# An RNN, a gated cell and their norms on one core: the second pass regrouped into tiles of one batch and eight steps

## The chip, the cores and the metric

The kernel runs on 1 core of one Trainium2 chip. The metric is the device time of one execution in microseconds (us). Engines are named PE (TensorE), DVE (VectorE), ACT (ScalarE), POOL (GpSimd) and SP (SyncE, which issues all DMAs here).

## The reference, cut to what matters

```python
mod = (_silu(c) @ wmod).reshape(8, 6, 1, 256)          # sa, ca, ga, sb, cb, gb
ga = (2 * (ga >= 0) - 1) * jnp.maximum(jnp.abs(ga), 0.25)   # the same for gb
h = _layernorm(x) * (1 + ca) + sa                      # x is [8, 1024, 256] float32
xb = h @ B.T
# over 1024 time steps, for 8 batches at once:
s = jnp.tanh(s @ A.T + xb_t);  y_t = s @ C.T
x = x + ga * (_layernorm(y + h) * gamma + beta)
h = _layernorm(x) * (1 + cb) + sb
# over the 8 batches as a scan, for all 1024 positions at once, c starts at in_c:
ft = sigmoid(h @ wf.T + c @ uf.T + bf);  it = sigmoid(h @ wi.T + c @ ui.T + bi)
gt = tanh(h @ wc.T + c @ uc.T + bc);     c = ft * c + it * gt
x = x + gb * jnp.tanh(h @ wo.T + c_final @ uo.T + bo)
```

## The kernel before, in words

The 1024 steps are cut into K=16 chunks of L=64 steps. One column of a tile is one (batch, chunk), so a step of the recurrence treats 8 x 16 = 128 columns. Since the chunks run side by side, the kernel makes a first pass to find each chunk's starting state, and a second pass that computes the output; a test at the end repeats both if a starting state was not good enough.

**First pass** (`unit1`, 36 units, one pair of steps each). Every unit norms two steps of x, adds the shift (POOL L511), transposes them (PE L1120), writes them to `h_park` in HBM, multiplies them by B (PE L1102, 12 matmuls) and keeps the result in `state`. From step `SKIP`=8 on, 28 units also carry two steps of the recurrence: PE L1062, DVE add L794, ACT tanh L612.

**Second pass** (`unit2`, 53 units). Unit u runs recurrence steps 2u and 2u+1 (u < 32), multiplies the states by C (L1164 in float32, L1173 from unit 10 in three high and low part products), adds `htok` (DVE L859) and norms the result twice (`bn_stats`, `bn_aggr`, reciprocal root as `ve` and a power on POOL L554/L556 and L546/L548). The transposes (L1253) put the features on the partitions; ACT L673 and DVE L909 write their high and low parts into the rings `hi` and `lo`. After eight pairs (GROUP=8) have been collected, the units from G0=11 on do the gates, one batch of 256 positions each: three gates of 12 matmuls from `hi`/`lo` (`gate_x`) and 12 from the cell state (`gate_c`, not for the first batch), all in L1136; ACT L705 applies the nonlinearities, POOL L532 and DVE L955, L854 form the new cell state `cst`, ACT L668 and DVE L864 its high and low parts `chi`, `clo`. From O0=19 on a unit multiplies one pair by wo (L1136, 12 matmuls), adds (DVE L936), takes tanh (ACT L693), scales by gb (POOL L567), transposes back (PE L1241, 4 transposes) and adds into `state` (DVE L947), which SP stores. In the first three groups of gates this is spread over the gate units of the next group; the last group's follows after the last gates.

The order of work on each engine is the order in which `unit2` of that engine names it; nothing is reordered at run time. Loops of two units are used in the stretches where all units are alike (`walk`), with registers in the addresses; the other units are written out. `has(u, first, n)` means first <= u < first + n.

Of the kernel before, what the change touches and what calls it, by code (L numbers as in the profile page):

```python
# [3 lines left out]

class At:
# [5 lines left out]
    def lin(self, k, c0=0):  # L21

        c = k * self.c + c0
        return c if isinstance(self.i, int) else self.i * (2 * k) + c

    def half(self, k, back, c0=0):

        c = k * ((self.c - back) // 2) + c0
        return c if isinstance(self.i, int) else self.i * k + c


def adaln_kernel(nc, x, A, B, C, gamma, beta, wf, uf, bf, wi, ui, bi, wc, uc, bc, wo, uo, bo, in_c, cond, wmod, out):
# [7 lines left out]
    P = 128  # L40
# [4 lines left out]
    SKIP = 8  # L45
# [34 lines left out]
    with ctx:  # L80
# [5 lines left out]

# [25 lines left out]
        hi = sb("hi", [P, 2, H, NB, GC], f32r)  # L112
        lo = sb("lo", [P, 2, H, NB, GC], f32r)
        xin = sb("xin", [P, 2, W])
        htok = sb("htok", [P, 2, W])
        h2tok = sb("h2tok", [P, W])
        y = sb("y", [P, W])[:, :]
        ow = sb("ow", [P, W])[:, :]
        pre = sb("pre", [P, D])
        hs = sb("hs", [P, 2, H, P])  # L120
        hs_hi = sb("hs_hi", [P, 2, H, P], f32r)
        hs_lo = sb("hs_lo", [P, 2, H, P], f32r)
        h_skip = sb("h_skip", [P, D])
# [45 lines left out]
        ga = state[:, at:at + D]  # L169
        gmag = state[:, at + D:at + 2 * D]  # L170
        gs = state[:, at + 2 * D:at + 2 * D + H * NB].rearrange("p (k b) -> p k b", k=H)
        gm = state[:, at + 3 * D:at + 3 * D + H * NB].rearrange("p (k b) -> p k b", k=H)
# [6 lines left out]
        BANK = dict(zip(NAMES, (psI, psG, psI, psG, psO, psI, psG, psO, psI, psG, psO)))  # L179

        def place(name):


            before = [i for i in range(NAMES.index(name)) if BANK[NAMES[i]] is BANK[name]]
            last = before[-1] if before else None
            return last, sum(n in whi for n in NAMES[:last + 1]) if before else 0

        def nth_split(name):

            return sum(n in whi for n in NAMES[:NAMES.index(name)])  # L190

        def whole(name):


            if name == "B":
                return state[:, 0:W].rearrange("p (k d) -> p k d", k=H)
            if name == "C":
                return ow.rearrange("p (k d) -> p k d", k=H)
            return (cst, uvec)[LATE.index(name) % 2][:, :, :]

        def ow_of(u):
            return ow if u < TAIL else (y, h2tok[:, :], ow)[(u - TAIL) % 3]

        def psW_of(u):
            return psW if u < TAIL else (psF, psG, psW)[(u - TAIL) % 3]

        def psO_of(u):
            return psO if u < TAIL else (psI, psO)[(u - TAIL) % 2]  # L210

        def back_of(u):

            back = 1 if u <= TAIL else 2
            return back if has(u, O0 + back, PAIRS) and u != TAIL + 1 else None

# [3 lines left out]
        q_w = {n: sem("q_w_" + n) for n in NAMES}  # L220
# [7 lines left out]
        q_wlo = sem("q_wlo")  # L228
        q_sig = sem("q_sig")
# [5 lines left out]
        q_tables = sem("q_tables")  # L235
        q_uc0 = sem("q_uc0")
# [1088 lines left out]
```

## Time and profile before

| | |
|---|---|
| median of 3 runs | 633.06 us (632.99 to 633.32) |
| the profiled execution, span from first to last instruction | 630.0 us |
| what lies around the span, median less span | 3.1 us |
| PE busy | 597.1 us, 95% |
| DVE, ACT, POOL busy | 462.2, 306.2, 368.7 us |
| HBM read and written | 29.90 and 16.78 MB, 74 GB/s over the span |

A page's busy time is the union of the spans of the instructions of an engine; it counts neither semaphore waits nor the issuing of DMAs. The matmuls of the page overlap in the pipeline, so what one costs is read from the distance between two starts in the timeline.

### The profile page before, as it was taken

The numbers are of one execution on the slowest core, as the hardware profiler recorded it, in microseconds if no ns is written. First come the engines' busy times: TensorE is split into PE (matmuls) and PEld (weight loads), VectorE is DVE, ScalarE is ACT, GpSimd is POOL, SyncE is SP. The second block draws the span as 40 slices with busy tenths as digits, with TensorE's granted clock in tenths as the row PEclk, the third lists the DMA queues.
The fourth block names the chain that finished last, engine by engine and source line by source line (L and its number), as shares of the span: only waits on it lengthen the run. The fifth ranks groups of instructions, "written<-read, shape, count | busy, mean of one in ns | idle before, by whom it ended". The sixth has DMA issues, their size and how long they took to land.

```text
span 630.0 us, 15433 instructions
## 1 busy us (share of the span) xinstructions
PE 597.1 (95%) x4840; PEld 580.0 (92%) x4840; DVE 462.2 (73%) x1143; ACT 306.2 (49%) x781; POOL 368.7 (59%) x479
## 2 busy tenths in 40 slices
PE   6699999999778899999999999999999999999995
PEld 3699999998668799999999999999999999999994
DVE  4799999956999988788778877777887672333335
ACT  2477777764443446535444454444445344333332
POOL 3666666643887576766676667776667533222234
PEclk9699999999999999999999999999999999999998
DMA  6644444432322212111111112111112000000003
GB/s 216 185 134 133 133 134 146 142 130 69 102 84 79 62 62 63 38 33 53 47 34 53 52 57 81 63 51 52 51 50 67 19 18 34 35 17 33 17 35 133
DMA packets 28557, 47.25 MB, mean 75 GB/s; under 512 B 4184, under 2 KB 7264, under 8 KB 28512
## 3 DMA queue, kind: packets, MB, share of 16 engines
q1 hardware_dynamic: 28512, 46.69, 22.9%
q8 instruction: 24, 0.39, 0.3%
q14 instruction: 21, 0.17, 0.1%
HBM read 29.90 MB, written 16.78 MB: 74 GB/s over the span
## 4 chain that ended last, share of the span: by engine, by line
PE 70%; DVE 10%; issue 9%; POOL 7%; DMA 1%; ACT 1%; SPq 0%; POOLq 0%; DVEq 0%; ACTq 0%
PE psF L1136 11%; PE psG L1136 11%; PE psI L1136 11%; PE psR L1062 10%; PE psW L1136 5%; PE psF L1062 4%; PE psC L1173 4%; PE psO L1102 4%; PE psW L1102 3%; PE psO L1241 1%; DVE state L917 1%; PE psT L1253 1%; POOL h2tok L526 1%; POOL gi L532 1%; DVE cst L854 1%
## 5 line engine op out<-in xcount | busy, mean ns | idle before, releaser
L1062 PE MATMUL psR<-hs,AT 128*128 128x128 f32 x648 | 109.0, 282 | 0.0
L1062 PEld LDWEIGHTS psR<-hs,AT 128*128 128x128 f32 x648 | 90.2, 194 | 3.5 <-ACT hs L650 0.2
L854 DVE TENSOR_TENSOR cst<-gf,gi 128x512 f32<-128x512 f32 x32 | 27.7, 865 | 62.9 <-POOL gi L532 62.9
L532 POOL TENSOR_TENSOR gi<-gi,gg 128x512 f32<-128x512 f32 x32 | 41.3, 1290 | 43.7 <-ACT gg L705 43.5
L567 POOL TENSOR_TENSOR ow<-ow,gbT 128x256 f32<-128x256 f32 x52 | 31.3, 622 | 60.8 <-ACT ow L693 60.8
L511 POOL TENSOR_TENSOR htok<-htok,uvec 128x256 f32<-128x256 f32 x64 | 46.1, 741 | 35.2 <-ACT htok L637 35.2
L1062 PE MATMUL psF<-hs,AT 128*128 128x128 f32 x312 | 61.2, 278 | 0.0
L518 POOL TENSOR_TENSOR hs_lo<-hs,hs_hi 128x256 fp32r<-128x256 f32 x44 | 42.5, 966 | 29.2 <-ACT hs_hi L658 29.1
L608 ACT ACTIVATE hs<-pre 128x256 f32<-128x256 f32 x42 | 17.6, 418 | 81.5 <-DVE pre L788 81.4
L955 DVE TENSOR_TENSOR gf<-gf,cst 128x512 f32<-128x512 f32 x28 | 28.7, 1027 | 33.2 <-ACT gf L705 33.2
L539 POOL TENSOR_TENSOR xin<-xin,gab 128x512 f32<-128x512 f32 x32 | 47.3, 1477 | 5.3 <-DMA xin<-in_L_attn_x_dram 5.3
L526 POOL TENSOR_TENSOR h2tok<-h2tok,sbt 128x512 f32<-128x512 f32 x32 | 48.9, 1528 | 0.0
L1062 PEld LDWEIGHTS psF<-hs,AT 128*128 128x128 f32 x312 | 48.3, 195 | 0.1
L917 DVE SCALAR_TENSOR_TENSOR state<-y,rstd,xin 128x256 f32<-128x256 f32 (+1 forms) x64 | 43.5, 718 | 0.4 <-POOL rstd L556 0.4
L612 ACT ACTIVATE hs<-pre 128x128 f32<-128x128 f32 x112 | 29.0, 305 | 29.4 <-DVE pre L794 29.3
L830 DVE SCALAR_TENSOR_TENSOR htok<-xin,mv,uvec 128x256 f32<-128x256 f32 x64 | 40.7, 674 | 1.8 <-DMA h_park<-htok 1.3
L668 ACT ACTIVATE chi<-cst 128x512 fp32r<-128x512 f32 x28 | 17.7, 632 | 49.9 <-DVE cst L854 49.9
L1136 PE MATMUL psI<-hi,wiT_hi 128*128 (+1 forms) x128 | 38.3, 299 | 0.0
L1136 PE MATMUL psF<-hi,wfT_hi 128*128 (+1 forms) x128 | 38.2, 298 | 0.0
L673 ACT ACTIVATE hi<-psT 128x256 fp32r<-128x256 f32 (+1 forms) x64 | 20.8, 377 | 33.5 <-PE psT L1253 33.5
L864 DVE TENSOR_TENSOR clo<-cst,chi 128x512 fp32r<-128x512 f32 x28 | 29.1, 1039 | 9.9 <-ACT chi L668 9.3
L1136 PE MATMUL psF<-hi,wfT_lo 128*128 (+1 forms) x128 | 36.3, 284 | 0.0
(255 smaller groups left out, 2326.9 us busy)
## 6 DMA issues: line engine op xcount, KB each, us to landing
xin<-in_L_attn_x_dram SPq DMA_DIRECT2D x64, 256.0 KB, 2.8
h_park<-htok SPq DMA_DIRECT2D x32, 256.0 KB, 2.0
htok<-h_park SPq DMA_DIRECT2D x32, 256.0 KB, 3.0
out_dram<-state SPq DMA_DIRECT2D x32, 256.0 KB, 2.0
state<-in_L_wmod_dram SPq DMA_DIRECT2D x3, 512.0 KB, 6.1
state<-in_L_attn_B_dram SPq DMA_DIRECT2D x1, 256.0 KB, 4.9
state<-in_L_attn_A_dram SPq DMA_DIRECT2D x1, 256.0 KB, 5.3
state<-in_L_attn_C_dram SPq DMA_DIRECT2D x1, 256.0 KB, 7.1
```

The lines of the kernel that those rows point to most:

```text
L511: pool.tensor_tensor(h, h, sa, ALU.add).then_inc(a_h, 1)
L518: pool.tensor_tensor(hs_lo[:, tt, :, :], hs[:, tt, :, :], hs_hi[:, tt, :, :].bitcast(f32), ALU.subtract).then_inc(s_hsl, 1)
L526: pool.tensor_tensor(h2, h2, sbt[:, :].rearrange("p (o d) -> p o d", o=1).broadcast_to([P, 2, D]), ALU.add).then_inc(s_h2, 1)
L532: pool.tensor_tensor(gi[:, :, :], gi[:, :, :], gg[:, :, :], ALU.mult).then_inc(s_ig, 1)
L539: pool.tensor_tensor(xg, xg, gab[:, :].rearrange("p (o d) -> p o d", o=1).broadcast_to([P, 2, D]), ALU.add).then_inc(s_xg, 1)
L567: pool.tensor_tensor(o4, o4, g4, ALU.mult).then_inc(s_ob, 1)
L830: dve.scalar_tensor_tensor(halfw(dst, tt), halfw(src, tt), mv[:, tt, 0:1], ca1, ALU.subtract, ALU.mult).then_inc(a_tmp, 1)
L854: dve.tensor_tensor(cst[:, :, :], gf[:, :, :], gi[:, :, :], ALU.add).then_inc(s_c, 1)
L917: dve.scalar_tensor_tensor(row(v.lin(1, -1), tt * D, D), halfw(y, tt), rstd[:, tt:tt + 1], halfw(xin[:, bk, :], tt), ALU.mult, ALU.add).th ...
L1062: ins = pe.matmul(ps, AT[:, k, m * P:(m + 1) * P], hs[:, 1 - tt, k, :], start=(k == 0 and (apart or m == 0)), stop=(k == H - 1 and (apart ...
L1102: last = pe.matmul(ps[:, m * 2 * P:(m + 1) * 2 * P], w["B"][:, k, m * P:(m + 1) * P], h[:, (ref - back) % 2, k * 2 * P:(k + 1) * 2 * P], s ...
L1136: last = pe.matmul(ps[:, at + m * columns:at + (m + 1) * columns], w[name][:, k, m * P:(m + 1) * P], xx(k), start=(start and n == 1), stop ...
```

## The change

A tile of the second pass is now one batch and 16 steps of all 16 chunks (`TB`=16, two halves j of `HT`=8 steps), 256 positions with the positions on the partitions, so that batch rows and outputs need no regrouping. The state of the recurrence is kept for four steps in `hs` and its parts for 16 steps in `hsh`, `hsl`; a C product (`project`) takes two batches and eight steps. The lags are CL=4 (C product), ML=8 (first norm), XL=10 (gates), OL=19 (output); NU=32 tiles, units 0 to 52, all written out. The product with wo follows in the gate unit itself, with the positions on the output's partitions, and waits in `wx` (11 buffers) for the cell's last state; the transposes back are gone. The identity matmuls that added `xb` (L1067) become DVE adds in units 0 to 9. Scale and shift of the second norm move into the copies after the transposes (`cb1T`) and into the biases (`shifts()` in unit 8: 6 and 72 matmuls). The norms' affine work moves from DVE to ACT (`zn`, `xn2`) and POOL (`zn` times a row). Rows of one batch come by broadcast DMAs from `rows_d`. All weights are loaded in the first pass. SKIP is 16: 24 of the 36 units of the first pass carry the recurrence, units 6 to 29.

The diff, cut to the order of the work on each engine. Four `unit2` follow one another: POOL's, ACT's, DVE's and PE's. What is left out of ACT's ahead of `step(2 * u + 1)`: tanh of step 2u, a late weight's copy, `xn2` (two, after `s_nB`), `chi` (after `s_c`), the tanh of `wx` (after `s_ua`); at its end the gates' sigmoids and tanh. Left out of DVE's ahead of `cst`: `nmB` (after `s_rB`), the add of step 2u, a late weight's difference; behind `x1`: `bn_stats` into `stB` and `bn_aggr` into `mvB`, each waiting for the one before.

```diff
-    SKIP = 8
+    SKIP = 16
-    LOADS = {1: ["B", "A", "wmod", "C"], 2: ["affine"], 3: ["wf"], 4: ["wi"], 5: ["wc"], 6: ["bias"]}
+    LOADS = {1: ["B", "A", "wmod", "C"], 2: ["affine"], 3: ["wf"], 4: ["wi"], 5: ["wc"], 6: ["bias"],
+             7: ["uf"], 8: ["ui"], 9: ["uc", "tabs"], 10: ["wo"], 11: ["uo"]}
...
+            def unit2(u):
+                if has(u, ML + 1, NU):
+                    m = u - ML - 1
+                    pool.wait_ge(s_mvB, 2 * m + 2)
+                    pool.tensor_tensor(veB[:, :], mvB[:, :, 1], epst[:, :], ALU.add).then_inc(s_veB, 1)
...
+                    pool.tensor_tensor(rstdB[:, :], veB[:, :], mhalf[:, :], ALU.pow).then_inc(s_rB, 1)
+                if has(u, XL + 1, NU):
...
+                    pool.wait_ge(s_g, 2 * n + 2)
+                    pool.tensor_tensor(gi[:, :, :], gi[:, :, :], gg[:, :, :], ALU.mult).then_inc(s_ig, 1)
+                if has(u, OL, LAST):
...
+                    pool.tensor_tensor(t, t, uvec[:, :], ALU.add).then_inc(s_ua, 1)
+                if has(u, ML, NU):
...
+                    pool.tensor_tensor(xg, xg, both(tA[:, m % 2, D:W]), ALU.add).then_inc(s_xg, 1)
+                    pool.wait_ge(s_mvA, 2 * m + 2)
+                    pool.tensor_tensor(veA[:, :], mvA[:, :, 1], epst[:, :], ALU.add).then_inc(s_veA, 1)
...
+                    pool.tensor_tensor(rstdA[:, :], veA[:, :], mhalf[:, :], ALU.pow).then_inc(s_rA, 1)
+                if has(u, 0, PAIRS):
+                    pool.wait_ge(s_hsh, u + 1)
...
+                    pool.tensor_tensor(pair_of(hsl[:, j], t), pair_of(hs, 2 * u % 4), pair_of(hsh[:, j], t).bitcast(f32),
+                                       ALU.subtract).then_inc(s_hsl, 1)
+                if has(u, ML, NU):
...
+                    pool.wait_ge(s_zn, 2 * m + 2)
+                    pool.tensor_tensor(two(zn[:, :]), two(zn[:, :]), both(tA[:, m % 2, 0:D]), ALU.mult).then_inc(s_zg, 1)
+                if has(u, OL, NU):
...
+                    pool.tensor_tensor(t, t, both(tG[:, o % 2, :]), ALU.mult).then_inc(s_ob, 1)
...
+            def unit2(u):
...
+                if has(u, 0, PAIRS):
+                    step(2 * u + 1)
...
+                    act.activation(pair_of(hsh[:, j], t), pair_of(hs, 2 * u % 4), ACT.Copy).then_inc(s_hsh, 1)
+                if has(u, XL - 1, NU):
...
+                    act.wait_ge(s_T, m + 1)
+                        act.activation(hi[:, m % 2, k, :], psT[:, k * POS:(k + 1) * POS], ACT.Copy,
+                                       scale=cb1T[:, k, m % NB:m % NB + 1]).then_inc(s_hi, 1)
+                if has(u, ML, NU):
+                    act.wait_ge(s_nA, m + 1)
+                        act.activation(zn[:, j * D:(j + 1) * D], tiles_of(m)[:, j, :], ACT.Identity, bias=nmA[:, j:j + 1],
+                                       scale=rstdA[:, j:j + 1]).then_inc(s_zn, 1)
...
+            def unit2(u):
...
+                if has(u, XL + 1, NU):
+                    dve.wait_ge(s_ig, n + 1)
+                    dve.tensor_tensor(cst[:, :, :], gf[:, :, :], gi[:, :, :], ALU.add).then_inc(s_c, 1)
+                if has(u, CL, 8 * NT):
+                    dve.tensor_tensor(z, (psC, psO)[c % 2][:, :], hin[:, c % 3, :], ALU.add).then_inc(s_z, 1)
+                        dve.bn_stats(stA[:, T % 2, 2 * (b + i) + j, :], halfw(z, i)).then_inc(s_stA, 1)
+                if has(u, XL + 1, NU) and (u - XL - 1) % NB < NB - 1:
+                    dve.tensor_tensor(clo[:, :, :], cst[:, :, :], chi[:, :, :].bitcast(f32), ALU.subtract).then_inc(s_clo, 1)
+                if has(u, OL + 1, NU):
+                    dve.tensor_tensor(tiles_of(o), tiles_of(o), two(wx[:, o % NWX, :]), ALU.add).then_inc(s_fin, 1)
+                if has(u, 0, PAIRS):
+                    step(2 * u + 1)
+                if has(u, ML, NU):
+                        dve.bn_aggr(mvA[:, j, :], stA[:, m // NB % 2, 2 * (m % NB) + j, :]).then_inc(s_mvA, 1)
+                if has(u, XL - 1, NU):
+                    dve.wait_ge(s_hi, 2 * m + 2)
+                        dve.scalar_tensor_tensor(lo[:, m % 2, k, :], psT[:, k * POS:(k + 1) * POS], cb1T[:, k, m % NB:m % NB + 1],
+                                                 hi[:, m % 2, k, :].bitcast(f32), ALU.mult, ALU.subtract).then_inc(s_lo, 1)
+                if has(u, ML, NU):
+                    dve.wait_ge(s_rA, m + 1)
+                    dve.scalar_tensor_tensor(nmA[:, :], mvA[:, :, 0], -1.0, rstdA[:, :], ALU.mult, ALU.mult).then_inc(s_nA, 1)
+                if has(u, XL, NU):
+                    dve.tensor_tensor(two(wx[:, n % NWX, :]), two(psW[:, :]), both(tW[:, n % 2, :]), ALU.add).then_inc(s_wx, 1)
+                if has(u, ML, NU):
+                    dve.wait_ge(s_zg, m + 1)
+                    dve.tensor_tensor(tiles_of(m), two(zn[:, :]), two(xin[:, m % 2, :]), ALU.add).then_inc(s_x1, 1)
...
+                if has(u, XL, NU):
+                    dve.wait_ge(s_f, 2 * n + 2)
+                    dve.tensor_tensor(gf[:, :, :], gf[:, :, :], prev, ALU.mult).then_inc(s_fc, 1)
...
+            def unit2(u):
...
+                    step(2 * u)
+                    late(u)
+                    project(u - CL)
+                    gate_x(n, 0)
+                    gate_x(n, 1)
+                    step(2 * u + 1)
+                    tokens(n + 1)
+                    gate_x(n, 2)
+                    times_uo(n // NB - 1)
+                    times_wo(n)
+                    shifts()
+                        gate_c(n, i)
```

## Rows read from the trace of the kernel before

**Rows 1.** The page, busy time, share of the span and instructions of each engine.

```profile
PE 597.1 (95%) x4840; PEld 580.0 (92%) x4840; DVE 462.2 (73%) x1143; ACT 306.2 (49%) x781; POOL 368.7 (59%) x479
```

**Rows 2.** Busy time by stretch: PE, weight loads, DVE, ACT, POOL; PE clock, DMA share, GB/s.

```profile
160.00:180.00 20.00, 16.39 (x120) 14.58 (x120) 19.89 (x53) 10.26 (x30) 16.32 (x21) 1.00 0.39 120
340.00:360.00 20.00, 20.00 (x174) 20.00 (x173) 16.77 (x42) 8.34 (x21) 13.46 (x17) 1.00 0.13 41
```

**Rows 3.** Timeline of PE, one full unit: start, duration, line, op, out<-in, count.

```profile
402.31 0.28 PE L1136 MATMUL psF<-chi,ufT_hi 128*128 128x256 f32 x1
...
406.57 1.05 PE L1062 MATMUL psR<-hs,AT 128*128 128x128 f32 x8
407.38 0.37 PE L1173 MATMUL psC<-CT_hi,hs_hi 128*128 128x256 f32 x1
...
409.65 0.60 PE L1241 MATMUL psO<-ident,ow 128*128 128x128 f32 x4
410.00 0.36 PE L1136 MATMUL psF<-hi,wfT_hi 128*128 128x256 f32 x1
...
423.69 0.60 PE L1241 MATMUL psO<-ident,ow 128*128 128x128 f32 x4
```

**Rows 4.** Timeline of DVE, ACT and POOL, same unit; the last row from the groups by shape.

```profile
409.76 0.69 DVE L859 TENSOR_TENSOR y<-psC,htok 128x512 f32<-128x512 f32 x1
409.88 0.63 ACT L668 ACTIVATE chi<-cst 128x512 fp32r<-128x512 f32 x1 [0.73 <-DVE cst L854]
...
412.15 0.24 DVE L872 BATCH_NORM_AGGREGATE mvb<-stb 128x2 f32<-128x6 f32 x2
412.31 0.72 DVE L878 BATCH_NORM_STATS2 st<-y 128x6 f32<-128x256 f32 x2
412.47 0.20 POOL L546 TENSOR_TENSOR ve<-mvb,epst 128x2 f32<-128x2 f32 x1 [0.79 <-DVE mvb L872]
412.74 0.70 POOL L548 TENSOR_TENSOR rstdb<-ve,mhalf 128x2 f32<-128x2 f32 x1
...
414.83 0.41 DVE L788 TENSOR_TENSOR pre<-psR,state 128x256 f32<-128x256 f32 x1
415.17 0.74 DVE L909 TENSOR_TENSOR lo<-psT,hi 128x256 fp32r<-128x256 f32 x2
415.36 0.42 ACT L608 ACTIVATE hs<-pre 128x256 f32<-128x256 f32 x1 [2.56 <-DVE pre L788]
...
416.14 0.90 ACT L690 ACTIVATE h2tok<-h2tok,rstdb 128x256 f32<-128x256 f32 x2
...
421.82 1.29 POOL L532 TENSOR_TENSOR gi<-gi,gg 128x512 f32<-128x512 f32 x1 [0.17 <-ACT gg L705]
...
L673 ACT ACTIVATE hi<-psT 128x256 fp32r<-128x256 f32 x36 | 11.8, 378 | 27.5 <-PE psT L1253 27.5
```

**Rows 5.** Timeline: a DVE operation with two SBUF inputs beside a POOL operation.

```profile
410.40 1.28 POOL L539 TENSOR_TENSOR xin<-xin,gab 128x512 f32<-128x512 f32 x1
410.61 1.62 DVE L864 TENSOR_TENSOR clo<-cst,chi 128x512 fp32r<-128x512 f32 x1 [0.17 <-ACT chi L668]
```

**Rows 6.** Timeline and chain, PE: the second pass's start, and the c0 block.

```profile
139.82 0.38 PE L1062 MATMUL psR<-hs,AT 128*128 128x128 f32 x2
...
196.12 0.22 PE psR L1062 x2
...
198.32 4.20 PE psW L1136 x36
202.52 0.63 PE psR L1062 x2
```

**Rows 7.** Timeline of DVE: first and last of 32 cell states, last output add.

```profile
230.57 1.13 DVE L854 TENSOR_TENSOR cst<-gf,gi 128x512 f32<-128x512 f32 x1 [1.61 <-POOL gi L532]
...
606.40 0.69 DVE L854 TENSOR_TENSOR cst<-gf,gi 128x512 f32<-128x512 f32 x1 [3.34 <-POOL gi L532]
...
625.20 0.69 DVE L947 TENSOR_TENSOR state<-psO,state 128x512 f32<-128x512 f32 x1 [1.23 <-PE psO L1241]
```

More of the change, by code:

```diff
@@ L119, in adaln_kernel @@
+        gf = sb("gf", [P, H, POS])
+        gi = sb("gi", [P, H, POS])
+        gg = sb("gg", [P, H, POS])
+        cst = sb("cst", [P, H, POS])
+        chi = sb("chi", [P, H, POS], f32r)
+        clo = sb("clo", [P, H, POS], f32r)
+        uvec = sb("uvec", [P, W])
+        tA = sb("tA", [P, 2, W])
+        tW = sb("tW", [P, 2, D])
+        tG = sb("tG", [P, 2, D])
         pre = sb("pre", [P, D])
-        hs = sb("hs", [P, 2, H, P])
-        hs_hi = sb("hs_hi", [P, 2, H, P], f32r)
-        hs_lo = sb("hs_lo", [P, 2, H, P], f32r)
@@ L146, in adaln_kernel @@
         again = sb("again", [1, 1], i32)
-        EARLY = ["B", "A", "C"]
-        NAMES = EARLY + LATE
+        htok = hin
+        st = stA[:, 0, 0:2, :]
+        mv, ve, rstd = mvA, veA, rstdA
+        whi["B"], wlo["B"] = chi, clo
+        sbE_hi, sbE_lo = chi[:, :, 0:P], clo[:, :, 0:P]
+        ca1, sa = uvec[:, 0:D], uvec[:, D:W]
+        hmT_hi, hmT_lo = (r[:, 0, 0, :, :, :].rearrange("p (i c) t k -> p i (c t k)", i=2) for r in (hsh, hsl))
         at = RAW * W
@@ L168, in adaln_kernel @@
         at += W
[L169 to L172, printed above, removed]
+        ga, gmag, gs, gm = (state[:, at + i * D:at + (i + 1) * D] for i in range(4))
         def bank(name):
@@ L178, in adaln_kernel @@
             "psR", "psC", "psT", "psF", "psI", "psG", "psW", "psO"))
[L179 to L190, printed above, removed]
-        def whole(name):
[L195 to L215, printed above, removed]
+        BANK = {"B": psI, "A": psG, "C": psI}
+        LBANK = (psG, psW, psI)
+        def whole(name):
+            return (state[:, 0:W] if name == "B" else zn[:, :]).rearrange("p (k d) -> p k d", k=H)
         q_ident = sem("q_ident")
         q_table = sem("q_table")
-        q_w = {n: sem("q_w_" + n) for n in NAMES}
+        q_w = {n: sem("q_w_" + n) for n in EARLY + LATE}
         q_wm = [sem(f"q_wm{j}") for j in range(3)]
@@ L408, in load @@
                                  allow_slow_non_contiguous=True).then_inc(q_bias, 16)
+                elif what == "tabs":
+                    sp.wait_ge(q_tab, 16)
+                    for i in range(3):
+                        sp.dma_start(rows_d[:, i, :], rows[0:P:K, i, :]).then_inc(q_rows, 16)
                 else:
@@ L1288, in unit2 @@
-                gate_c(1)
-                gate_c(2)
+                if x and n % NB:
+                    for i in range(3):
+                        gate_c(n, i)
             def body():
```

1072 lines of the change are left out of this document (552 added, 520 removed).

## The prediction, made before the changed kernel was run

> **What bounds the kernel now.** I read the page's busy times first: PE stands at 95% of the span, no other engine above 73% [rows 1]. Then the busy times by stretch, to see where that isn't so: between 160 and 180 us, in the first units of the second pass, DVE is busy 19.89 of 20 us and PE only 16.39; by 340 us PE is busy all the time at full clock, and DVE has 3 us of slack, POOL 6.5 [rows 2]. The timeline of PE shows one full gate unit from 409.65 to 423.69, so 14.04 us, back to back [rows 3]: 36 products of a gate pass take 4.26 (402.31 to 406.57), a recurrence step 0.81, the four transposes back 0.35, and the product behind such a group starts some 0.09 late. The gates run from the first cell state at 230.57 to the last at 606.40, 375.8 us [rows 7]: that is the bulk, and PE sets it. The profiled execution spans 630.0 us and the median is 633.06, so 3.1 us come on top of any span below.
>
> **What the change does to PE.** Transposes back: 4 per pair, 0.35 + 0.09 = 0.44 us, gone 32 times: -14 us where PE sets the pace. The full unit then takes 14.04 - 0.44 = 13.60. A first-batch unit has no `gate_c` (-4.26), and units 18, 26 and 34 add the uo product (about 1.75, an estimate from its 4 float32 matmuls at twice the columns of half a recurrence step's 4). Units without recurrence save 1.8, without C product 1.42 (12 at a third of 4.26). From unit 11 to 41 PE's work sums to 13.6 x 21 + 11.8 x 4 + 10.4 x 6 - 3 x 4.26 + 3 x 1.75 = 387.7. It is more than the 375.8 before, since the first group's wo products, once behind the gates, now stand in front.
>
> **What paces a unit then.** The order on DVE, ACT and POOL is fixed, so I follow what each waits for in a full unit, from one cell state to the next. All durations from [rows 4] but for the cell state's 0.69 [rows 7]; "to" is the 0.03 to 0.17 between an end and the start that it releases.
> (a) DVE: cst 0.69, z (as y L859) 0.69, to 0.16, statistics 0.72, clo 0.69, output add 0.69 (two SBUF inputs, as cst), add of step 2u+1 0.41: 4.15 with gaps. chi on ACT is hidden by z and its statistics.
> (b) ACT: to 0.12, tanh 0.42, hsh 0.63 (512 elements, as chi), hi 0.72 (two of 0.378); DVE: to 0.15, lo 0.86, nmA 0.17: 3.15. The mean's way (aggregate 0.24, ve 0.20, power 0.70) runs beside it.
> (c) ACT: to 0.12, zn 0.90 (as L690, two); POOL: to 0.07, zn times row 1.28; DVE: to 0.10, x1 0.69: 3.16.
> (d) DVE: to 0.16, statistics 0.74, aggregate 0.34: 1.24.
> (e) POOL: to 0.08, ve 0.20, to 0.07, power 0.70; then gi times gg 1.29 and 0.10 to the next cst: 2.44. The power stands ahead of the gate product in POOL's queue, so the next cell state waits for this unit's norm. That closes the ring.
> Sum 14.15 us a unit, more than PE's 13.60, though no engine is busy more than about 10 of them.
>
> **Where two engines meet.** A `clo` that starts while POOL is at a 1.28 us operation takes 1.62 instead of 0.69: POOL's ends at 411.68, DVE's 0.55 later, at 412.23 [rows 5]; so a DVE operation with two SBUF inputs finishes 0.55 after POOL's end. In the ring this comes three times. POOL goes from gi straight to the uvec add (or the `xg` add), 0.1 ahead of cst: +1.05. It goes from the zn product straight to the gb product, ahead of x1: +1.05. And DVE goes from the aggregate straight to gf, ahead of ve: +0.55. Bounds: nothing to 2.65; I take all, since in each case both are ready at that instant. Ring: 16.8 us a unit.
> The Trainium skill (SBUF - State Buffer, two separate sides) calls the pair of ports that VectorE and GpSimd share an exclusive lock, held by who starts first; the rows agree in the end time, and by a bandwidth split instead the ring would stay nearer 15.5.
>
> **The sum over the gate units.** Units 19 to 31: 13 x 16.8 = 218.4. Units 11 to 18 have no output add (-0.7) and no gb product (-1.05): 8 x 15.05 = 120.4. Units 32 to 35 without recurrence: (b) shrinks to lo and nmA behind the power, -2.0: 4 x 14.8 = 59.2. Units 36 to 39 without z, but with the wait for chi (0.63 and two gaps): 4 x 14.1 = 56.4. Units 40, 41 have no first norm, PE sets 10.6: 21.2. Three units without clo: -2.2. Together 473.4 from the first cell state to the last, against 375.8: **+97.6**.
>
> **Ahead of it.** First pass: four units (30 to 33) drop the recurrence. Each drops four DVE adds of at most 0.41 and 1.6 of PE, but its chain ve, power, scale, two shifts on POOL stays at some 3.4 of the 3.8 us that a unit takes: 0 to 6.6 in all, I take -2.5. Five more weights (256 KB each) and `tabs` on SP's queue I cost at nothing: SP only issues, and the copies are wanted 15 units later; if the link were full, about 1 us each. The second pass starts at 139.82 [rows 6], so now at 137.3. Units 0 to 3: one step is PE 0.8, two half adds, two half tanh, then the weight's copy and difference stand between the steps: 3.85 each. Units 4 to 7 add the C product between the steps and z, statistics on DVE behind it: 5.4 each. Unit 8: step, C product, step, then `shifts`. The 36 tiny c0 products took 4.20 [rows 6], so 78 take some 9.2, and the granted clock suffers: the pair of recurrence matmuls behind the c0 block took 0.63 and not 0.22. Unit 8 is 12.6 with 1 for that clock. Units 9 and 10 run the ring's parts (a) to (e) without the cell state: 11.5 each. To the first cell state at unit 11, with (e): 15.4 + 21.4 + 12.6 + 23 + 2.5 = 75, so 212.3 against 230.57: **-18.3**. DVE's three full norm operations that moved to ACT and POOL are part of that gain.
>
> **Behind it.** Last cell state to the end is 23.6 now [rows 7]. Then: cst 0.7, uo 1.9, its copy 0.7, first add 0.8, tanh and gb product 2.1, and eight outputs each with two DVE adds and one POOL product that exclude each other (0.69 + 0.69 + 1.28, less where tanh hides: 2.5 each), last add to the end 4.1 as today (625.89 to 630.0): 29. **+5.3**.
>
> Span 212.3 + 473.4 + 29 = 714.7; time 717.8, say **718 us**, 13% slower.
>
> **Unrolling.** PE is busy 20.00 of 20 us in the looped stretch [rows 2], so loops cost no time there and writing them out gives none. The Trainium skill (Runtime: NRT & Kernel Launch, instruction fetch mechanics) says a taken branch outside the window stalls on a fetch; by it the looped stretches would give back perhaps a few us; this trace shows no such gap on PE.
>
> **Rivals.**
> 1. The ring closes within PE's time (something I put in series runs beside it, so the ring is under 13.6): PE stays the bound. Units 11 to 41 take 387.7, the ramp stays near 75 or, if its ring parts are shorter too, 62, the end 25: span 137.3 + 62 to 75 + 387.7 + 25 = 612 to 625, time 615 to 628. It would be **faster**. For it: PE is at 95% today and loses 14 us of work; DVE loses two norm passes. Against it: the ring needs only seven handovers with durations measured here, and even without meeting POOL it sums to 14.15. It decides at a mean of 12.6 us per unit for the 31 units (630 less what lies around them).
> 2. The ring is there, but the meetings cost less (POOL's next operation comes after DVE's, or the lock is short): 14.15 in units 19 to 31, PE's 13.6 in 11 to 18, 12.1 and 11.4 in 32 to 39: 184 + 109 + 48 + 46 + 21 = 408, and an end of 25: span 645, time 648. With one of the meetings, 665 to 690.
> 3. The DMAs are late: twice as many rows of 1 KB, and three broadcasts a unit, some 1.3 MB. At 16 us a unit that is 80 GB/s, and the stretch from 160 us moves 120 [rows 2]; loads are issued a unit or two ahead. If they were late the time would be above 740.
> 4. The change does nothing to the pace, gains and losses cancel within 0.2%, about what a measurement of this kernel can tell from no change.
>
> **How the numbers follow.** The ring with its meetings 0.55 (own range 695 to 738), the ring with fewer of them 0.23 (645 to 695), PE-bound 0.16 (612 to 630), late DMAs or more 0.04, no difference 0.02. The range 648 to 738 leaves out the PE-bound case and the tail above. Faster is rival 1, 0.16; same 0.02; slower is the rest, 0.82.
>
> **What would show it.** PE's busy share near 80% and long regular gaps on PE in front of `gate_c`, ended by DVE clo; a unit of 16 to 17 us between two `cst`; `cst` and `x1` at about 1.7 us each where POOL is at an add; POOL's gi product starting right behind the power, and long after ACT's last tanh; the first `cst` near 212 us. Wrong if units are 13.6 us apart with PE back to back, or if gi waits for ACT's gg as today (421.82, idle ended by ACT [rows 4]).

## The result and the profile after

The changed kernel takes 718.28 us (median of 4 runs, 716.79 to 720.45) beside 633.19 for the kernel before on the same chip: a ratio of 1.135 (95% interval 1.1328 to 1.1373), 85 us slower. The profiled execution took 716.79 us and spans 715.0; TensorE's mean granted clock is 0.924 (before 0.982).

The page of the kernel after: busy time, share of the span and instructions; then the chain that ended last, by engine; then groups of PE, DVE and POOL with their idle time before and what ended it.

```profile
PE 592.8 (83%) x4650; PEld 571.7 (80%) x4650; DVE 477.1 (67%) x1062; ACT 340.7 (48%) x804; POOL 394.9 (55%) x453
...
POOL 32%; issue 25%; PE 17%; DVE 15%; ACT 5%; DMA 3%; SPq 2%; POOLq 0%; DVEq 0%; ACTq 0%
...
L1128 PE MATMUL psR<-hs,AT 128*128 128x128 f32 x432 | 69.6, 295 | 42.3 <-ACT hs L655 32.5
...
L878 DVE TENSOR_TENSOR cst<-gf,gi 128x512 f32<-128x512 f32 x32 | 49.9, 1560 | 7.6 <-POOL gi L549 6.9
...
L865 DVE SCALAR_TENSOR_TENSOR nmB<-mvB,rstdB 128x2 f32<-128x2 f32 x32 | 37.5, 1172 | 25.4 <-POOL rstdB L544 25.4
L581 POOL TENSOR_TENSOR wx<-wx,tG 128x512 f32<-128x512 f32 x32 | 41.8, 1308 | 20.1 <-DMA tG<-rows_d 11.6
```

PE has 4 us less work than before [rows 1] in 85 us more, and its recurrence matmuls (L1128) alone have 42.3 us of idle time ahead of them, 32.5 of it ended by ACT. No engine is near its limit; "issue" and POOL hold the chain. The cell add takes 1.56 us in the mean, and `nmB`, an operation on two columns, 1.17.

The busy times by stretch say the same of the middle (columns as in [rows 2]). PE waits, its clock dips, and no other engine is full.

```profile
400.00:420.00 20.00, 15.47 (x127) 15.06 (x127) 14.27 (x25) 9.27 (x21) 14.15 (x14) 0.97 0.34 104
440.00:460.00 20.00, 16.87 (x137) 16.29 (x136) 12.62 (x25) 10.63 (x26) 13.23 (x13) 1.00 0.30 92
```

One unit, from a cell add (L878) to the next: 497.16 to 513.08, 15.92 us. DVE's timeline (start, duration, line, op, out<-in, count, idle before and what ended it):

```profile
497.16 1.50 DVE L878 TENSOR_TENSOR cst<-gf,gi 128x512 f32<-128x512 f32 x1
...
503.64 0.88 DVE L919 SCALAR_TENSOR_TENSOR lo<-psT,cb1T,hi 128x256 fp32r<-128x256 f32 x2 [1.80 <-ACT hi L691]
504.43 0.15 DVE L925 SCALAR_TENSOR_TENSOR nmA<-mvA,rstdA 128x2 f32<-128x2 f32 x1
...
507.11 1.76 DVE L934 TENSOR_TENSOR state<-zn,xin 128x512 f32<-128x512 f32 x1 [1.92 <-POOL zn L575]
509.01 0.75 DVE L938 BATCH_NORM_STATS2 stB<-state 128x6 f32<-128x256 f32 x2
509.94 0.25 DVE L943 BATCH_NORM_AGGREGATE mvB<-stB 128x2 f32<-128x6 f32 x2 [0.17 <-DVE stB L938]
510.10 0.66 DVE L950 TENSOR_TENSOR gf<-gf,cst 128x512 f32<-128x512 f32 x1
511.62 1.21 DVE L865 SCALAR_TENSOR_TENSOR nmB<-mvB,rstdB 128x2 f32<-128x2 f32 x1 [0.86 <-POOL rstdB L544]
512.75 0.41 DVE L857 TENSOR_TENSOR pre<-psR,state 128x256 f32<-128x256 f32 x1
513.08 1.50 DVE L878 TENSOR_TENSOR cst<-gf,gi 128x512 f32<-128x512 f32 x1
```

POOL's in the same unit, and one row of ACT's:

```profile
505.79 1.28 POOL L575 TENSOR_TENSOR zn<-zn,tA 128x512 f32<-128x512 f32 x1 [1.55 <-ACT zn L698]
507.03 1.29 POOL L581 TENSOR_TENSOR wx<-wx,tG 128x512 f32<-128x512 f32 x1
510.26 0.55 POOL L541 TENSOR_TENSOR veB<-mvB,epst 128x2 f32<-128x2 f32 x1 [1.95 <-DVE mvB L943]
510.89 0.69 POOL L544 TENSOR_TENSOR rstdB<-veB,mhalf 128x2 f32<-128x2 f32 x1
511.55 1.26 POOL L549 TENSOR_TENSOR gi<-gi,gg 128x512 f32<-128x512 f32 x1
512.76 1.26 POOL L555 TENSOR_TENSOR wx<-wx,uvec 128x512 f32<-128x512 f32 x1
```

```profile
507.04 0.85 ACT L714 ACTIVATE gg<-psG,biasT 128x256 f32<-128x256 f32 x2
```

The reader should see three things. ACT finishes `gg` at 507.89, and POOL takes it up only at 511.55, since `veB` and the power stand ahead in its queue and wait for the norm's statistics. `x1` (L934) and `cst` (L878) take 1.76 and 1.50 us where POOL has just begun an operation of its own. And `nmB` is held from 511.62 to 512.83 by `gi` on POOL.

The second pass in four stretches, in us (before from [rows 6, 7]; after from the timelines of PE and DVE):

| stretch | before | after | difference |
|---|---|---|---|
| start of the pass | 139.82 | 141.42 | +1.6 |
| to the first cell add | 90.75 | 83.79 | -7.0 |
| first to last cell add | 375.8 | 453.5 | +77.7 |
| to the end | 23.6 | 36.3 | +12.7 |
| span | 630.0 | 715.0 | +85.0 |

### The profile page after: what moved, and what is told of

It is laid out like the page before. It is cut to its first block, busy times and chain, and to the rows that moved or that the text cites. A ratio compares the mean times of both kernels' runs of the same rounds, so it can differ in the third digit from the quotient of the medians.

```text
span 715.0 us, 13830 instructions
## 1 busy us (share of the span) xinstructions
PE 592.8 (83%) x4650; PEld 571.7 (80%) x4650; DVE 477.1 (67%) x1062; ACT 340.7 (48%) x804; POOL 394.9 (55%) x453
## 4 chain that ended last, share of the span: by engine, by line
POOL 32%; issue 25%; PE 17%; DVE 15%; ACT 5%; DMA 3%; SPq 2%; POOLq 0%; DVEq 0%; ACTq 0%
POOL zn L575 6%; POOL gi L549 6%; POOL xin L561 4%; POOL wx L581 4%; POOL wx L555 3%; DVE cst L878 3%; POOL hsl L570 3%; POOL veB L541 2%; PE psR L1061 2%; PE psO L1092 2%; PE psF L1061 2%; POOL rstdA L566 2%; DVE hin L835 2%; PE psW L1092 2%; PE psW L1243 1%
## 5 line engine op out<-in xcount | busy, mean ns | idle before, releaser
L1128 PE MATMUL psR<-hs,AT 128*128 128x128 f32 x432 | 69.6, 295 | 42.3 <-ACT hs L655 32.5
L1128 PEld LDWEIGHTS psR<-hs,AT 128*128 128x128 f32 x432 | 58.4, 201 | 49.4 <-ACT hs L655 36.9
L934 DVE TENSOR_TENSOR state<-zn,xin 128x512 f32<-128x512 f32 x32 | 44.6, 1395 | 56.5 <-POOL zn L575 56.5
L575 POOL TENSOR_TENSOR zn<-zn,tA 128x512 f32<-128x512 f32 x32 | 41.1, 1286 | 48.0 <-ACT zn L698 48.0
L531 POOL TENSOR_TENSOR hin<-hin,uvec 128x256 f32<-128x256 f32 x64 | 46.5, 748 | 34.3 <-ACT hin L642 34.3
L570 POOL TENSOR_TENSOR hsl<-hs,hsh 128x512 fp32r<-128x512 f32 x32 | 41.0, 1282 | 33.7 <-ACT hsh L684 32.2
L878 DVE TENSOR_TENSOR cst<-gf,gi 128x512 f32<-128x512 f32 x32 | 49.9, 1560 | 7.6 <-POOL gi L549 6.9
L581 POOL TENSOR_TENSOR wx<-wx,tG 128x512 f32<-128x512 f32 x32 | 41.8, 1308 | 20.1 <-DMA tG<-rows_d 11.6
L561 POOL TENSOR_TENSOR xin<-xin,tA 128x512 f32<-128x512 f32 x32 | 50.4, 1574 | 0.0
L1161 PE MATMUL psG<-hi,wcT_hi 128*128 128x256 f32 x128 | 43.4, 339 | 0.0
L835 DVE SCALAR_TENSOR_TENSOR hin<-xin,mvA,uvec 128x256 f32<-128x256 f32 x64 | 40.9, 679 | 2.4 <-DMA h_park<-hin 0.8
L1161 PE MATMUL psG<-lo,wcT_hi 128*128 128x256 f32 x128 | 40.2, 314 | 0.0
L1161 PE MATMUL psG<-hi,wcT_lo 128*128 128x256 f32 x128 | 40.1, 313 | 0.0
```

The source lines that it names most:

```text
L531: pool.tensor_tensor(h, h, sa, ALU.add).then_inc(a_h, 1)
L561: pool.tensor_tensor(xg, xg, both(tA[:, m % 2, D:W]), ALU.add).then_inc(s_xg, 1)
L570: pool.tensor_tensor(pair_of(hsl[:, j], t), pair_of(hs, 2 * u % 4), pair_of(hsh[:, j], t).bitcast(f32), ALU.subtract).then_inc(s_hsl, 1)
L575: pool.tensor_tensor(two(zn[:, :]), two(zn[:, :]), both(tA[:, m % 2, 0:D]), ALU.mult).then_inc(s_zg, 1)
L581: pool.tensor_tensor(t, t, both(tG[:, o % 2, :]), ALU.mult).then_inc(s_ob, 1)
L835: dve.scalar_tensor_tensor(halfw(dst, tt), halfw(src, tt), mv[:, tt, 0:1], ca1, ALU.subtract, ALU.mult).then_inc(a_tmp, 1)
```

## The experiments

All ran beside the kernel before, on the same chip as the others of their set. In the table is the median of 4 runs (7 for the first pass alone), and the ratio to the kernel before with its 95% interval. The kernel after has 718.28 and 1.135. Places in a trace are those of one profiled execution, so a few us of difference in the median need not all be found there.

| kernel | us | ratio |
|---|---|---|
| 1 ring reordered | 697.71 | 1.1011 (1.097 to 1.1053) |
| 2 gb product first | 717.94 | 1.1338 (1.1303 to 1.1374) |
| 3 hi first | 724.38 | 1.1435 (1.1398 to 1.1471) |
| 4 after, less of wo | 718.60 | 1.1362 (1.1317 to 1.1408) |
| 5 gb first, nm by scalars | 697.61 | 1.1038 (1.0991 to 1.1086) |
| 6 = 1 with 5 | 667.80 | 1.0568 (1.0497 to 1.064) |
| 7 before, first pass of the change | 629.24 | 0.9938 (0.9915 to 0.9962) |
| 8 after, shifts mostly left out | 712.32 | 1.1242 (1.1216 to 1.1269) |
| 9 bo's row later | 713.98 | 1.1253 (1.1216 to 1.129) |
| 10 last gamma rows early | 712.07 | 1.1228 (1.1194 to 1.1263) |
| 11 = 6, 9 and 10 | 661.11 | 1.0439 (1.0403 to 1.0475) |
| 12 before, less of wo | 625.52 | 0.9872 (0.9842 to 0.9901) |

**1. The order on POOL, DVE and ACT.**

```diff
 POOL
+   gi * gg            (waits for ACT's i and g)
    veB, rstdB         (wait for mvB)
-   gi * gg
 DVE
-   nmB                (waits for rstdB)
    pre (step 2u), cst
+   nmB
    z, statistics, clo
 ACT
+   chi                (waits for cst)
    xn2 (two, wait for nmB)
-   chi
```

> Three entries of the serial queues change places in the second pass, no work is added or left out: POOL multiplies i by g ahead of the variance and rstd of LayerNorm B; DVE's two-column nmB goes from the head of the unit to just behind the cell add; ACT copies chi ahead of the normalisation of the other batch. Theory (a ring through the in-order queues of DVE, ACT and POOL paces a unit, 15.94 us, and PE with 13.6 us of work does not): the path gates -> gi -> cell add -> chi -> gates loses about 1.7 us, the units 19 to 31 fall to 14.3, the units with no LayerNorm B meeting to about 13.7, some 39 us in all: 679 us. Rival, PE or its lower clock sets the unit: 716 to 720, no change. Rival, late loads set it: no change either. Rival, only the operation that is held longest matters and another takes its place at once: 705 to 715.

Measured 697.71 us, 21 less, where 679 was forecast. Most profiled cell adds are 14.20 us apart in units 19 to 31, against 15.94: the forecast 14.3 for that piece held, and with it the claim that `veB` and the power in front of `gi` lengthened the ring; PE's work is the same. The other half of the forecast failed: units 11 to 18 stayed at 14.2 instead of 13.7 and units 32 to 37 rose from some 14.0 to between 14.0 and 16.2. The chain of this kernel (start, duration, what) from 247 us on shows why: two queues now close another ring, gates, `gi`, `veB`, the power, a held `nmB`, `xn`, PE's transposes and gates.

```profile
247.25 0.85 ACT gg L714 x2
...
248.32 1.64 issue
249.96 0.19 POOL veB L546
250.23 1.12 POOL rstdB L549
251.37 1.24 DVE nmB L878
252.63 1.10 ACT xn L671 x2
...
253.78 0.66 PE psT L1196 x4
```

**2. One exchange on POOL.**

```diff
+   wx * tG            (gb product, output)
    zn * row           (waits for ACT's zn)
-   wx * tG
```

> One exchange on POOL: the output's product with tG goes ahead of LayerNorm A's product with the table row, so that POOL no longer works on two SBUF inputs while DVE wants to add x1. Theory (the ring runs through x1 and what stands behind it on DVE): x1 falls from 1.76 to about 0.7 us in 21 units (19 to 39), each unit 1.1 shorter, 23 us in all: 695 us. Rival, DVE's waits at x1 are slack that PE fills: 716 to 720. Rival, PE paces the unit: the same, 716 to 720.

Measured 717.94: nothing, the intervals overlap. Read alone this would speak for the first rival. DVE's timeline of this kernel, and POOL's, say something else:

```profile
503.99 1.08 DVE L925 SCALAR_TENSOR_TENSOR nmA<-mvA,rstdA 128x2 f32<-128x2 f32 x1
...
507.60 0.69 DVE L934 TENSOR_TENSOR state<-zn,xin 128x512 f32<-128x512 f32 x1 [1.93 <-POOL zn L581]
```

```profile
503.76 1.29 POOL L577 TENSOR_TENSOR wx<-wx,tG 128x512 f32<-128x512 f32 x1
506.28 1.29 POOL L581 TENSOR_TENSOR zn<-zn,tA 128x512 f32<-128x512 f32 x1 [1.23 <-ACT zn L698]
```

`x1` fell from 1.76 to 0.69 us as forecast, and the meeting moved: the gb product, started earlier, now holds `nmA`, 1.08 us for two columns instead of 0.15, with all of `zn` behind it. The units are 15.8 long.

**3. hi ahead of the hidden state's copy on ACT.**

```diff
+   hi (two, wait for psT)
    hsh copy
-   hi
```

> One exchange on ACT: the rounding of the new tile to hi goes ahead of the copy of the hidden state for the next project. Theory (the ring includes hi, since PE's gates wait for it): about 0.6 us less in 21 units, 11 us in all: 706 us. If hi is not on the ring, or PE paces: 716 to 720.

Measured 724.38, 6 us slower, units of 16.2. The same thing again: `hi` comes earlier, so that `lo` starts 5.83 us behind the cell add instead of 6.48, but `hsl` on POOL, which needs `hsh`, comes later and lies over `nmA`, which then takes 1.07 us (DVE's timeline of this kernel, and POOL's).

```profile
509.89 1.07 DVE L926 SCALAR_TENSOR_TENSOR nmA<-mvA,rstdA 128x2 f32<-128x2 f32 x1
```

```profile
509.65 1.29 POOL L570 TENSOR_TENSOR hsl<-hs,hsh 128x512 fp32r<-128x512 f32 x1 [0.64 <-ACT hsh L693]
```

**4 and 12. A third of wo's products left out, in the kernel after and in the kernel before.**

```diff
-                        for h, w in ((hi, whi), (hi, wlo), (lo, whi)):
+                        for h, w in ((hi, whi), (lo, whi)):
```

> The kernel after, with the product of wo's rounding rest left out (4 of its 12 matmuls in every tile, 0.47 us of PE per unit; the output lacks that term). Theory (ring): PE has 2.3 us to spare in a unit, the time stays within 1 us of the kernel after: 717 to 718.5. Rival, PE's work or clock sets the unit: 32 x 0.47 = 15 us less, 703 us.

> The kernel before, with the same third of wo's products left out as in the kernel after (where it gave 0.0 us; the output lacks that term). Theory: in the kernel before PE sets the pace of the second pass, so that nearly all of 32 x 0.47 = 15 us shows: 618 to 621 us. Rival, a ring through the other engines binds before as well: 630 to 633.

In the kernel after the cut gave nothing (718.60), in the kernel before 8.4 us (625.52 beside 633.91). So PE's work is no longer on the path after the change, and it was before. But not all of the 15 us came out before: freed of them, PE waits there too, 37.02 us busy in a stretch of 40 (first fence below) where the kernel before has 40.00, and from 312 us on the chain of the cut kernel runs through ACT's gates, POOL's `gi`, DVE's norm and adds and POOL again.

The kernel before has this ring itself. Its chain is PE alone from 300 to 426 us, but from 427 to 514 us it runs mostly through POOL (five of its rows in the second fence: start, duration, what). Its cell adds in units 19 to 21 and 27 to 29 are 13.6 us apart, just as in the cut kernel, and only those in 22 to 25 take the 13.9 to 14.1 of PE's work, which the cut brings down to 13.6. So a full unit of the kernel before can't get under 13.6 us by less work on PE: its ring lies 0.4 us under PE's 14.04.

```profile
460.00:500.00 40.00, 37.02 (x310) 36.23 (x309) 30.32 (x72) 17.12 (x43) 25.18 (x32) 1.00 0.13 45
```

```profile
448.46 1.29 POOL gi L532
449.86 1.14 DVE cst L854
451.02 0.64 ACT chi L668
...
456.74 1.00 POOL hs_lo L518
...
462.08 1.29 POOL gi L532
```

**5 and 6. The small operations in a form that isn't held.** 5 is experiment 2 with `nmA` and `nmB` as below; 6 has the order of experiment 1 as well.

```diff
-   dve.scalar_tensor_tensor(nmB[:, :], mvB[:, :, 0], -1.0, rstdB[:, :], ALU.mult, ALU.mult)
+   for j in range(2):
+       dve.tensor_scalar(nmB[:, j:j + 1], mvB[:, j, 0:1], rstdB[:, j:j + 1], -1.0, ALU.mult, ALU.mult)
```

> The exchange of the run before (gb product ahead of the zn product on POOL) moved the meeting from x1 (1.76 to 0.69 us) to the two-column nmA (0.15 to 1.08 us), and the units stayed at 15.8. Here nmA and nmB are made by two tensor_scalar operations each (the mean times a per-partition scalar, so one SBUF input instead of two), with that exchange. Theory (DVE operations with two SBUF inputs are held while POOL runs one with two, and such a hold sits on the ring): nmA and nmB take 0.1 to 0.3 us in all and are not held, the gain at x1 stays, the units 19 to 31 fall from 15.9 to 14.8, some 1 us in 21 units and a little in the rest: 718 to about 695. Rival, the small operations are held in this form too: 715 to 718, units 15.8. Rival, the two scalar operations cost more than they save: 720 and over.

> The reordering that gave 697.7 us (gi ahead of rstdB on POOL, nmB behind the cell add, chi ahead of xn) with the gb exchange and with nmA and nmB as tensor_scalar operations. Its profile showed a new ring of 14.2 us: gates, gi, veB, rstdB, nmB held for 1.2, xn, PE's transposes and gates. Theory: nmB not held takes 1 us out of that ring, it falls under PE's own work, and PE sets the unit with 13.6 to 13.8 us: 30 units by 0.5 and 7 by up to 1.5 in the last third, 697 to about 680 us. Rival, the small operations are held in this form too, or PE's work already set the 14.2: 695 to 698.

Measured 697.61 and 667.80. With one tensor input, not two, two operations of one column each take 0.33 us together, also while POOL is at work, so the holds are gone. The edits do not add up singly: against the kernel after the exchange on POOL alone is worth nothing, with the two forms 21 us, the order alone 21 us, all together 50. What the forms are worth without the exchange wasn't run. Units 19 to 31 are 15.04 apart in 5, near the forecast of 14.8, and 13.35 in 6, where I had put 13.6 to 13.8. In 6 the ring is under PE's work: the chain of that kernel has PE alone between 440 and 480 us (five of its rows in the second fence; the first is DVE's timeline), and PE is busy 40.00 us from 340 to 380.

```profile
441.00 0.33 DVE L928 TENSOR_SCALAR nmA<-mvA,rstdA 128x1 f32<-128x1 f32 x2
```

```profile
449.66 0.44 PE psT L1200 x4
450.09 1.38 PE psG L1165 x12
451.48 1.36 PE psW L1214 x12
452.84 1.41 PE psF L1165 x12
...
457.08 0.89 PE psR L1132 x8
```

**7. The first pass of the change in the kernel before.**

```diff
-    SKIP = 8
-    RAW = 8
+    SKIP = 16
+    RAW = 12
```

(and the loop's cuts as in the change)

> The kernel before with the first pass of the change alone: its side work starts from step 16 instead of 8 and fewer states are kept raw; the second pass is that of before. Theory: the first pass gets shorter by less than one unit's side work, 1.5 to 2 us: 631.2 to 631.7. Rival, the first pass is set by PE's recurrence and projection alone: no change, 633.2. Rival, all of the skipped side work counted, 6.6 us less: 626.6. Rival, the start of the second pass moves later, as in the kernel after (141.4 against 139.8): 635.

Measured 629.24 beside 633.16, and this is the only complete version here that is faster than the kernel before: by 0.4 to 0.9%. The gain by the median, 3.9 us, is twice the forecast 1.5 to 2. Its profiled execution was among the slower of its runs (631.36 of 627.63 to 631.38): there the second pass starts at 138.70 instead of 139.82, 1.1 us earlier. Where the rest comes from isn't shown.

**8. The bias shift.** Of the 72 eight-column matmuls 66 are left out (so the biases are not shifted as they should be).

```diff
-  for name, shi, slo in ((wf/wi/wc, sbT_hi, sbT_lo), (uf/ui/uc, c0z_hi, c0z_lo)): 12 matmuls per column block
+  one matmul per column block
```

> The kernel after with 66 of the 72 eight-column matmuls of the bias shift left out before unit 8 (the biases of the second pass are not what the reference wants). Their profile: 10.3 us for the second half, a granted clock of 0.67 in the 20 us from 180 on and 0.82 in the next 20, and the first gates 12.9 us later than I forecast. Theory (the matmuls cost their time and the half clock behind them): the first cell add comes 12 to 15 us earlier, 704 to 706 us. Rival, the clock falls there for another reason, the pause of PE, so that only the matmuls' own time goes: 708 to 710. Rival, another chain (LayerNorm, hi) is as late as they: 712 to 718.

Measured 712.32, 6 us less instead of 12 to 15, and the first cell add at 221.27 instead of 225.21. PE's next recurrence pair starts at 195.44, with the matmuls at 195.12: it waits 7.1 us for ACT, whose input waits in DVE's queue behind `nmB`. So the chain through the second norm ends as late as the matmuls, and what came forward is the C product behind them, from 196.83 to 186.67.

The granted clock between 180 and 200 us is 0.67 in both (half speed, 1.2 GHz, for part of the stretch), but it doesn't follow that the matmuls have no part in it. From some 180 to 184 us it is half in both, ahead of the matmuls; in the 20 us before, PE was busy 13.77 us in the one and 13.95 in the other, and whether those gaps are the cause wasn't tried. After that the two differ. With the matmuls the clock is full until 190.2 us and then half until 200.4: in the middle of them, and with PE busy without a pause since 180.4, their starts go from 0.11 to 0.21 us apart (first fence). Without them PE pauses from 188.3 to 195.4, and it is half from about 191 us to 200.4. A pause has taken their place, so the cause of that second fall stays open. The first two fences are from the kernel after, the others from this one.

```profile
190.11 0.25 PE L1243 MATMUL psW<-sbT_hi,wcT_hi 128*128 128x8 f32 x1
190.22 0.35 PE L1243 MATMUL psW<-sbT_lo,wcT_hi 128*128 128x8 f32 x1
190.43 0.35 PE L1243 MATMUL psW<-sbT_hi,wcT_lo 128*128 128x8 f32 x1
```

```profile
180.00:200.00 20.00, 19.59 (x121) 19.62 (x122) 6.29 (x19) 3.85 (x10) 7.05 (x9) 0.67 0.16 46
```

```profile
180.00:200.00 20.00, 12.30 (x73) 12.05 (x74) 9.54 (x26) 5.90 (x16) 8.82 (x12) 0.67 0.15 46
```

```profile
195.44 0.79 PE L1128 MATMUL psR<-hs,AT 128*128 128x128 f32 x2 [7.11 <-ACT hs L652]
```

**9. bo's row later in the first pass.**

```diff
-                    for dst, src in ((gamma_b, gamma), (beta_b, beta), (bo_b, bo)):
+                    for dst, src in ((gamma_b, gamma), (beta_b, beta)):
...
-             7: ["uf"]
+             7: ["bo", "uf"]
```

> The kernel after, with the broadcast of bo (128 KB) issued in unit 7 of the first pass instead of unit 2, where it stood ahead of the first x tile. In the kernel after, x landed 7.26 us after its issue and at 23.5, in the kernel before at 20.6, and the second pass began at 141.4 instead of 139.8. Theory: the first pass gets its 2.9 us back, the second pass begins at 138.5 to 139.2, 2.2 to 2.9 us less: 715.5 to 716. Rival, the first pass makes the late start up before its end: 718.

Measured 713.98, 4 us less than the kernel after. The second pass begins at 138.60, 2.8 us earlier, in the profiled execution; its first cell add comes 1.0 earlier, its span is 2.2 shorter. The broadcast of bo ahead of the first x tile (x landed 7.26 us after its issue, in 5.2 at most here) was what ate the gain of the shorter first pass. The kernel before has no such broadcast: it loads bo as 1 KB.

**10. The last six gamma rows early.**

```diff
+                if u == 38:
+                    sp.wait_ge(s_z, 8 * NT)
+                    six broadcasts rows_d -> hin
...
-                    pool.tensor_tensor(t, t, both(tG[:, o % 2, :]), ALU.mult)
+                    pool.tensor_tensor(t, t, both(row), ALU.mult)      # row in hin for the last six
```

> The kernel after, with the last six gamma rows of the output loaded early, into the tile hin that is no longer read by then, instead of one by one into the pair tG. Between the last cell add (678.69) and the end (715.0) the product on POOL waited for a row six times, 11.6 us in all. Theory: the drain falls from 36.3 us to 28 to 30, the time to 710 to 712. Rival, the drain is set by the rest of the chain (tanh, add, store): 716 to 718.

Measured 712.07, 6 us less; last cell add to the end 32.4 us instead of 36.3. The waits for the rows are gone, and my 28 to 30 was still too short: what is left is a cadence of 4.70 us for two tiles on POOL, each pair waiting 1.89 us for ACT's tanh, which waits for DVE's add, which waits behind an output add of 1.73. These are the rows of this kernel:

```profile
688.74 1.74 DVE L916 TENSOR_TENSOR state<-state,wx 128x512 f32<-128x512 f32 x1 [1.16 <-POOL wx L595]
...
691.82 2.81 POOL L595 TENSOR_TENSOR wx<-wx,hin 128x512 f32<-128x512 f32 x2 [1.89 <-ACT wx L691]
696.52 2.81 POOL L595 TENSOR_TENSOR wx<-wx,hin 128x512 f32<-128x512 f32 x2 [1.89 <-ACT wx L691]
```

**11. All of it.** No new lines, 6 with 9 and 10.

> All of the edits together: the reordered ring with unheld small operations (667.8 us, units of 13.35 us set by PE alone), bo's broadcast later and the last six gamma rows early. Theory: the gains add, since they lie in the three successive stretches: 667.8 less 2.5 less 7 = 658 us, and what is left over the kernel before (633) is the filling and draining of the second pass (80 and 28 us). Rival, the drain's rows come from the edge of the ring edit already: 663 to 666.

Measured 661.11, of a forecast 658. This is the best form of the second pass found here, 57 us faster than the kernel after and still 4.4% slower than the kernel before. In its profile the first cell add is at 217.95, the last at 627.12, the span 659.0: against the kernel before 12.6 us less ahead of the gates, 33.4 more between the cell adds and 8.3 more behind. Its units are 12.6 to 13.6 us up to unit 31. Units 19 to 31 are even shorter than before (172.6 against 178.5 us together), and 11 to 18, which now hold wo's products as well, are longer (105.7 against 95.8). The larger part of the 33.4 lies in units 32 to 41, 130.8 against 101.6: they take mostly 12.8 to 14.5 us each, the chain again goes through POOL's power, `xn` and PE, and the granted clock is 0.93 between 540 and 580 us. So most of what is left between the cell adds is the ring and the clock in the last ten units, not PE's work alone.

## Why the prediction was right

The time (718 against 718.28) and the span (714.7 against 715.0) came out nearer than the terms did: three errors of +12.9, -19.9 and +7.3 us cancel, and that is luck. The mechanism is the one given; the sizes need the list.

**The start.** "PE sets it", of the gates in the kernel before, holds only in part: a ring of 13.6 us stands right behind PE's 14.04 and paces six of its full units (12). The -14 us for the transposes was too much even for the old order: 15 us of PE's work gave 8.4 there.

**The ring.** Right, and shown: taking PE's work away does nothing (4), changing only the order takes 21 us (1), and with the holds gone as well PE sets the unit up to unit 31 (6). Size: 16.8 us a full unit forecast, 15.94 measured. By piece, forecast and measured: (a) 5.2 and 4.52, (b) 3.15 and 2.90, (c) 4.2 and 4.29, (d) 1.24 and 1.32, (e) 2.99 and 2.89. In (a), successive DVE operations overlap by about 0.08 us each in the trace, and `cst` took 1.50 and not 1.74: it starts 0.3 after POOL's uvec add, because a meeting that I had not listed stands before it. That is `nmB`, two columns, held until `gi` ends. I had priced it by its size. Units 11 to 18 were 14.2 in the mean (forecast 15.05), 32 to 35 14.1 and 36 to 39 13.7 (14.8, 14.1). Together the gates took 453.5 and not 473.4. Three durations of the sum are not in the rows that it names: lo 0.86 (0.74 there), nmA 0.17 and the aggregate's 0.34 (0.24 there); measured are 0.88, 0.15 and 0.25.

**The meetings.** All three were there: `x1` 1.76 us, `cst` 1.50, `veB` 0.55 instead of 0.20. They added 1.07, 0.81 and 0.35 us, 2.2 in place of 2.65. `x1` and `cst` ended 0.55 and 0.56 us after POOL's operation, as forecast (507.11 + 1.76 = 508.87, POOL's ended at 508.32). The 0.55 is not the same for every size: the two-column `nmB` ended 0.02 after POOL's `gi`, and POOL's `veB` 0.05 after DVE's `gf`. The Trainium skill (SBUF - State Buffer, two separate sides) has it that a DVE operation with two SBUF inputs and a GpSimd operation that reads SBUF exclude each other, and that the one that starts first holds the pair of ports for its whole length. The runs agree: `nmB` with two tensor inputs took 1.21 us, to the end of `gi`, and with one it took 0.33. What the prediction didn't say is that such a hold can't be priced one at a time: 2 and 3 each removed one delay and made another, in 2 nearly as large (1.07 and 0.93 us), in 3 larger (0.65 and 0.92).

**Ahead of the gates.** Wrong by 12.9 us (212.3 against 225.21), in three steps. "Each drops ... I take -2.5" was -1.1 in the kernel before (7, profiled start of the second pass); and bo's row, a load that the prediction's list leaves out, cost 2.8 us (9), so that the pass started 1.6 later instead of 2.5 earlier. "Unit 8 is 12.6 with 1 for that clock" was 17.1: step, C product and step took 5.9 us (178.16 to 184.07, the C product at half clock), where the sum leaves 2.4, and the 78 products of `shifts` 11.2 instead of 9.2 and 1, the 72 tiny ones 10.4 of it (184.83 to 195.26). Experiment 8 corrects my reason: their time held the first cell add up by 3.9 us only, since the chain through the second norm ends as late as they do. Units 9 and 10 with the wait for the first `cst` took 29.9, not 25.5; part of this is the half clock (0.82 granted between 200 and 220).

**Behind the gates.** Wrong by 7.3 us (29 against 36.3). The terms written there add up to 30.3, so 1.3 is the sum's own. "uo 1.9" was 3.78 (at 680.42), at a granted clock of 0.50 behind PE's wait of 4.10 us for `cst`. And for the rest the step that failed is "loads are issued a unit or two ahead". For `tG` with its two buffers that is as far ahead as POOL's products, and in the drain those can follow each other every 2.35 us (10), while a row takes 3.6 to land (the page's median). 10 took 3.9 of it back.

**The rivals.** PE-bound from the start was wrong as the kernel stood, but is what comes out up to unit 31 when order and holds are mended (6), and the time then is 668 and not 615 to 628: my PE sum of 387.7 was reached in no version, 409.2 in the best, since the last ten units stay with the ring (11). "No meetings" (648) left out that the first ring is closed by another one a little shorter (1). Late DMAs: in the gates none was seen.

## What to carry to other kernels

When a unit's length is no engine's busy time, write down for one unit what each in-order queue waits for, in the order of the queue, and look for an operation that is ready but stands behind one that isn't (here `gi` behind the power). Test the reading by taking work from the engine that was the bound: if nothing changes, the ring holds. And look at the timeline after each reordering before you call it useless: an exchange that gained 1.1 us at one place lost it at another until a two-column operation was written with one tensor input.

## What the runs showed that was not expected

- A DVE operation on 2 columns with two SBUF inputs took 1.21 us when POOL began its own 512-column operation first, 0.15 when not. As two operations with a per-partition scalar: 0.33 us, never held.
- TensorE's granted clock fell to half at 190.2 us in the middle of the tiny matmuls, though PE had not paused since 180.4. Without most of them it was half there too, but in and behind a pause of 7.1 us, so whether they bring it down is open.
- A 128 KB broadcast queued ahead of the first x tile moved the end of a 140 us pass by 2.8 us.
- The kernel before was less purely PE-bound than its 20.00 of 20 us of busy time suggest: of 15 us of PE work taken out it gave back 8.4, and six of its full units take 13.6 us with and without that work.
